# Four full-precision passes for two blocks of three early steps, x batches one step later, and two wide warming products

## The reference, cut to what matters

```python
def layer(x, adj, W, b):            # x 8192x128, adj 8192x8192, W 128x128, all float32
    h = jnp.maximum(_layernorm(x, axis=-1), 0.0)
    support = jnp.matmul(h, W)
    out = jnp.matmul(adj, support) + b
    return x + jax.nn.relu(out)
```

## Time and profile before

| | us |
|---|---|
| median of 3 runs | 722.28 (722.16 to 722.79) |
| the profiled execution | 722.6 |
| its span, first to last instruction | 720.8 |
| PE busy | 715.5 (99%) |
| PEld busy | 586.4 (81%) |
| DVE busy | 620.4 (86%) |
| ACT busy | 517.0 (72%) |
| POOL busy | 171.5 (24%) |
| DMA | 281.60 MB, mean 391 GB/s |

### The profile page before, as it was taken

The page is one execution under the profiler, slowest core; times in us unless marked ns, Lnnn a source line. Parts: engine busy times, 40 slices in busy tenths (PEclk is TensorE's granted clock), DMA queues, the critical chain, the costliest instruction groups (busy, mean ns, idle before and its releaser), DMA issues.

```text
span 720.8 us, 7916 instructions
## 1 busy us (share of the span) xinstructions
PE 715.5 (99%) x3125; PEld 586.4 (81%) x3125; DVE 620.4 (86%) x387; ACT 517.0 (72%) x394; POOL 171.5 (24%) x99
## 2 busy tenths in 40 slices
PE   9999999999999999999999999999999999999998
PEld 5788888888888888888888888888888888888886
DVE  5899999999999888988789888878888787888885
ACT  2798988888888867766567677677676676766662
POOL 4445455554444402222011000000000000033213
PEclk9999999999999999999999999999999999999999
DMA  9999999999999999999999999999999999999992
GB/s 352 408 409 407 408 412 415 412 416 415 416 414 416 418 415 412 398 374 402 373 412 392 408 409 389 377 401 383 386 392 373 389 394 387 391 404 397 366 400 85
DMA packets 45109, 281.60 MB, mean 391 GB/s; under 512 B 5136, under 2 KB 5776, under 8 KB 31504
## 3 DMA queue, kind: packets, MB, share of 16 engines
q1 hardware_dynamic: 44496, 280.25, 97.5%
q10 hardware_dynamic: 576, 0.85, 0.4%
HBM read 276.89 MB, written 4.19 MB: 390 GB/s over the span
## 4 chain that ended last, share of the span: by engine, by line
PE 97%; DMA 2%; DVE 0%; ACT 0%; SPq 0%; issue 0%; DVEq 0%
PE banks L558 94%; DMA raw<-adj 2%; PE banks L600 2%; PE banks L592 1%; PE banks L585 0%; PE banks L586 0%; PE banks L584 0%; ACT high L378 0%; SPq L244 0%; DVE x_sb L479 0%; DVE x_sb L487 0%; DVEq L150 0%; DVE warm L491 0%; DVEq L478 0%
## 5 line engine op out<-in xcount | busy, mean ns | idle before, releaser
L516 DVE TENSOR_TENSOR low<-raw,high 128x3072 fp32r<-128x3072 f32 (+2 forms) x255 | 574.7, 2276 | 86.4 <-PE banks L558 64.4
L378 ACT ACTIVATE high<-raw 128x3072 fp32r<-128x3072 f32 (+2 forms) x255 | 483.0, 1903 | 190.3 <-DMA raw<-adj 178.4
L558 PE MATMUL banks<-high,h_high 128*128 128x512 f32 x1012 | 271.6, 390 | 1.1 <-ACT high L378 1.1
L558 PE MATMUL banks<-high,h_low 128*128 128x512 f32 x1012 | 271.0, 389 | 0.0
L558 PE MATMUL banks<-low,h_high 128*128 128x512 f32 x1012 | 267.8, 389 | 0.0
L558 PEld LDWEIGHTS banks<-high,h_high 128*128 128x128 f32 x1012 | 189.8, 188 | 41.8 <-ACT high L378 2.0
L558 PEld LDWEIGHTS banks<-low,h_high 128*128 128x128 f32 x1012 | 189.8, 188 | 39.9 <-DVE low L516 0.4
L558 PEld LDWEIGHTS banks<-high,h_low 128*128 128x128 f32 x1012 | 189.9, 188 | 39.5
L330 POOL TENSOR_SCALAR x_sb<-x_sb,bias 128x512 f32<-128x512 f32 x16 | 49.5, 3095 | 419.3 <-DMA x_sb<-x_blocks 419.3
L321 POOL TENSOR_SCALAR z_sb<-x_sb,neg_mean,rstd 128x128 f32<-128x128 f32 x60 | 89.8, 1510 | 1.6
L306 POOL TENSOR_TENSOR rstd<-var_eps,minus_half 128x4 f32<-128x4 f32 (+2 forms) x17 | 31.6, 1861 | 118.3 <-DVE var_eps L421 109.1
(11 more groups left out here) (34 smaller groups left out, 50.1 us busy)
## 6 DMA issues: line engine op xcount, KB each, us to landing
raw<-adj SPq DMA_DIRECT2D x106, 1536.0 KB, 8.9
raw<-adj SPq DMA_DIRECT2D x82, 768.0 KB, 10.5
raw<-adj SPq DMA_DIRECT2D x69, 512.0 KB, 11.8
x_sb<-x_blocks SPq DMA_DIRECT2D x16, 256.0 KB, 8.6
out_blocks<-x_sb SPq DMA_DIRECT2D x15, 256.0 KB, 9.7
x_sb<-x SPq DMA_DIRECT2D x14, 256.0 KB, 11.9
raw<-adj SPq DMA_DIRECT2D x3, 256.0 KB, 6.9
raw<-adj ACTq DMA_DIRECT2D x1, 256.0 KB, 2.7
```

What stands on the lines that cost most here:

```text
L378: nc.scalar.activation(high[:, t % HIGH_SLOTS, cols], raw[:, t % RAW_SLOTS, cols], ACT.Copy).then_inc(high_ready, 1)
L516: nc.vector.tensor_tensor(low[:, t % LOW_SLOTS, cols], raw[:, t % RAW_SLOTS, cols], high[:, t % HIGH_SLOTS, cols].bitcast(F32), ALU.subtra ...
L558: return nc.tensor.matmul(banks[:, FIRST_BANK[g] + c, :], h[:, (t - FIRST_STEP[g]) * DEPTHS[g] + k, :], tile[:, slot, at:at + BANK], start ...
```

## The change

Six things change. In steps 5, 6 and 7 (`PART_WHOLE`) the third piece (blocks 4 and 5) is no longer halved by ACT and DVE (`halves_of` leaves it out of both loops and of the counts in `halved`); PE multiplies it raw by the whole tile in f32 (`with_whole`), between low 0 and low 1. The whole tiles 5 to 7 are made by one new DVE operation at the end of step 2, `h_part`, from `z_sb`. SP, when it loads into the slots of steps 5 to 7 (at steps 9 to 11), waits also for PE. Batches of x are loaded, and their means taken, at steps 6, 10, ... in place of 5, 9, ...; the squares move to steps 7 and 8, 11 and 12, ..., the variance to 8, 12, ...; batch 3 is rectified at step 5 in place of 7, and the later ones where they were. The halving of `h_first` moves from step 9 to step 28. The warming products are two of 448 columns in place of eight of 128, from a buffer that `last_sum` lends; ACT's first activation reads `minus_half` and waits for POOL in place of DVE.

```diff
@@ -35,7 +35,9 @@
-WARMING = 8
+
+PART_WHOLE = range(5, 8)
+WARMING, WARM = 2, 448
@@ -88,11 +90,16 @@
+def halves_of(t):
+
+    return range(len(split_of(t)) - (t in PART_WHOLE))
+
+
 def halved(t, i=None):
 
     while len(HALVED_BEFORE) <= t:
-        HALVED_BEFORE.append(HALVED_BEFORE[-1] + len(split_of(len(HALVED_BEFORE) - 1)))
-    return HALVED_BEFORE[t] + (len(split_of(t)) if i is None else i + 1)
+        HALVED_BEFORE.append(HALVED_BEFORE[-1] + len(halves_of(len(HALVED_BEFORE) - 1)))
+    return HALVED_BEFORE[t] + (len(halves_of(t)) if i is None else i + 1)
@@ -107,23 +114,24 @@
 def mean_at(t):
-    return batch_at(t, 1, 3) if t >= 5 else None
+    return batch_at(t, 2, 3) if t >= 6 else None
 
 
 def variance_at(t):
-    return batch_at(t, 3, 3) if t >= 7 else None
+    return batch_at(t, 0, 2) if t >= 8 else None
 
 
 def rectified_at(t):
-    return 2 if t == 2 else batch_at(t, 3, 2) if t >= 7 else None
+
+    return {2: 2, 5: 3}.get(t, batch_at(t, 3, 2) if t >= 11 else None)
 
 
 def squares_at(t):
 
-    j = batch_at(t, t % 4, 3) if t >= 6 and t % 4 in (2, 3) else None
-    if j is None:
+    j = batch_at(t, 3, 3) if t % 4 == 3 else batch_at(t, 0, 2)
+    if t < 7 or j is None:
         return None
-    at = BATCHES[j][0] + (t % 4 - 2) * 2
+    at = BATCHES[j][0] + (t % 4 == 0) * 2
     return j, range(at, at + 2)
@@ -268,6 +280,9 @@
+                if t - RAW_SLOTS in PART_WHOLE:
+
+                    sp.wait_ge(products_done, t - RAW_SLOTS + 1)
@@ -314,6 +329,8 @@
+                if j == 4:
+                    pool.wait_ge(h_part_ready, 1)
@@ -359,8 +376,8 @@
-            act.wait_ge(warm_ready, 1)
-            nc.scalar.activation(unread[:, :], warm[:, 0:1], ACT.Square)
+            act.wait_ge(constants_ready, 1)
+            nc.scalar.activation(unread[:, :], minus_half[:, 0:1], ACT.Square)
@@ -510,19 +527,25 @@
+                if t == 2:
+
+                    dve.wait_ge(products_done, 1)
+                    tiles = len(PART_WHOLE)
+                    nc.vector.tensor_scalar(h_part[:, 0:tiles * P], z_sb[:, x_slot(2) % Z_SLOTS, P:(1 + tiles) * P],
+                                            0.0, None, ALU.max).then_inc(h_part_ready, 1)
...
-                if t == 9:
+                if t == 28:
@@ -589,7 +612,7 @@
             for _ in range(WARMING):
-                nc.tensor.matmul(banks[:, PSUM_BANKS - 1, 0:P], warm[:, :], warm[:, :], start=True, stop=True)
+                nc.tensor.matmul(banks[:, PSUM_BANKS - 1, 0:WARM], warm[:, 0:P], warm[:, :], start=True, stop=True)
@@ -632,17 +655,29 @@
+
+                def with_whole(i):
+                    pe.wait_ge(h_part_ready, 1)
+                    pe.wait_ge(raw_landed[t % RAW_SLOTS][i], landed(t, i))
+                    at = (t - PART_WHOLE[0]) * P
+                    for c in blocks_of(t, i):
+                        nc.tensor.matmul(banks[:, FIRST_BANK[0] + c, :], h_part[:, at:at + P],
+                                         raw[:, t % RAW_SLOTS, c * BANK:(c + 1) * BANK], start=False, stop=False)
 
 
                 with_high(0)
                 if len(pieces) == 3:
                     with_high(1)
                     with_low(0)
-                    with_high(2)
-                    with_low(1)
-                    with_low(2)
+                    if t in PART_WHOLE:
+                        with_whole(2)
+                        with_low(1)
+                    else:
+                        with_high(2)
+                        with_low(1)
+                        with_low(2)
```

More of the change, by code:

```diff
@@ L170, in gnn_layer @@
         rstd = sb("rstd", [P, TILES])
-        warm = sb("warm", [P, P])
         unread = sb("unread", [P, 1])
@@ L183, in gnn_layer @@
         last_sum = sb("last_sum", [P, BANK])
+        warm = last_sum[:, 0:WARM]
+        h_part = last_sum
         banks = ctx.enter_context(nc.psum_tensor("banks", [P, PSUM_BANKS, BANK], F32))
@@ L197, in gnn_layer @@
         h_first_ready = sem("h_first_ready")
+        h_part_ready = sem("h_part_ready")
         early_high = sem("early_high")
@@ L374, in _ @@
                     act.wait_ge(high_used, t - HIGH_SLOTS - FOUR_PASS + 1)
-                for i in range(len(split_of(t))):
+                for i in halves_of(t):
                     cols = columns_of(t, i)
@@ L379, in _ @@
                                          ACT.Copy).then_inc(high_ready, 1)
-                    if i == (0 if t >= NARROW_UNTIL else len(split_of(t)) - 1) and rectified_at(t) is not None:
+                    if i == (0 if t >= NARROW_UNTIL else halves_of(t)[-1]) and rectified_at(t) is not None:
                         rectify(rectified_at(t))
@@ L625, in with_high @@
                             last = product(t, c, k, h_low, high, t % HIGH_SLOTS)
-                    if i == pieces[-1]:
+                    if i == halves_of(t)[-1]:
                         last.then_inc(high_used, 1)
```

## The result

| | before | after |
|---|---|---|
| median of 8 runs, us | 722.42 (722.15 to 722.79) | 726.51 (723.68 to 728.84) |
| the profiled execution, us | 722.6 | 728.84 |
| its span, us | 720.8 | 727.0 |

The change makes the kernel slower: ratio 1.0057, interval 1.0043 to 1.0071. The forecast was 722.1 us and no change, the range ended at 723.3. The runs also scatter over 5 us where those of before lie within 0.7.

What follows compares the result with a forecast made beforehand. PE was taken to bound the kernel. The terms +1.06 - 1.3 - 0.29 + 0.3 = -0.23 us gave 722.4 on the profiled 722.6 us, or 722.1 us against the median; range 721.4 to 723.3.

Steps and rivals of the forecast that it cites:

- What bounds the kernel, and the prize: PE is the bound; its stalls in steps 5 and 10 make the prize at most 1.6 us out of 722.
- Four passes, +1.06 us: Steps 5 to 7, last two blocks: six products of 0.858 us replace 0.681 us each, +1.06 us on PE.
- The step-5 stall, -1.3 us: Step 5: piece 2 is read as it lands, so PE's whole stall goes, -1.3 us.
- rival 1: Step 6: a lagging DMA engine makes piece 1 0.4 to 1.2 us late; 722.6 to 723.3 us, chance 0.15.
- `h_part` on DVE, +0.3 us: Ahead of step 3's subtractions: the new DVE operation reaches PE nearly whole, +0.3 us, bounds 0 and 0.8.
- The step-10 stall, -0.29 us: Step 10: PE's 0.29 us lost on low products goes, as the copies of h_first leave step 9.
- Warming: Kernel start: two wide products end before h_first is there; costs nothing if the clock still rises in time.
- Rival 2: Kernel start: the clock rises late, first products 0.86 us slower each; chance 0.09, 0.06 of it beyond two products.
- Moved steps: Statistics one step later: ACT waits some 0.5 us every fourth step, nothing on the path.
- Rival 3: Rectified tiles make PE wait or ACT hands its 0.5 us on; 722.1 plus 0.5 to 4.5 us, chance 0.04.

Runs made afterwards that it cites:

- a1: The changed kernel with x batches, means, squares and variances back at their old steps; 722.56 us, ratio 1.0005.
- w2: The changed kernel with the old schedule, four passes in step 5 alone and the eight narrow warming products; 721.95 us, ratio 0.9995.
- w1: The changed kernel with the old schedule and four passes in step 5 alone, wide warming kept; 722.04 us, ratio 1.0001.
- h1: The changed kernel with only the first 64 columns of each piece subtracted on DVE in steps 24 to 63; 722.50 us, ratio 1.0005.
- v1: The changed kernel with all four squares and the variance back at steps 7, 11, ..., loads and means left late; 722.89 us, ratio 1.0012.
- p2: The changed kernel with each DVE subtraction of steps 24 to 63 cut into two of half the width; 722.59 us, ratio 1.0008.
- a3: The changed kernel with rectification behind the last piece of its step, not the first, from step 24 on; median 725.2 us, ratio 1.0038.

## Why the prediction was wrong, by its own steps

- **What bounds the kernel, and the prize: right.** PE, two stalls of 1.6 us; both are gone. (Rows 3 hold two more waits of weight loads for ACT, 0.3 and 0.2 us before 20 us, which the prediction passed over.)
- **Four passes, +1.06 us: right.** The records of the new product stand 0.43 us apart, as in step 1, without a cost for entering or leaving them: the fourth starts at 31.87 us (from the same view), and the second product behind it at 32.53, which is 0.43 + 0.23 us later.
- **The step-5 stall, -1.3 us: right in its size; which part removed it is open.** The packet of instructions moved as the prediction thought it might: it lies between 28 and 30 us before and between 32 and 34 us in the changed kernel, where nothing waits for it. In a1 it has moved too, so that a1 has no wait there doesn't single out the four passes. With the wide warming alone (g1) it lies between 30 and 32 us, step 5 has no stall, and PE stands 0.60 us in step 6 instead. Nothing came in step 6 of the changed kernel (rival 1), but rival 1's waits are real in g1 and w2.
- **`h_part` on DVE, +0.3 us: right in kind.** The instruction took 0.35 us, and of that 0.17 reached PE in step 3.
- **The step-10 stall, -0.29 us: right.**
- **Warming: nothing, about right.** The memset of 448 columns took 0.43 us and the first real product came 0.35 us later, hidden behind the landing at 8.5 us. Rival 2's mechanism is real (9.79 us in w1) but isn't what made this change slow.
- **Moved steps: this is the step that failed.** It read POOL's batch as 8.0 us long, moved it by one step, found ACT waiting 0.5 us and called that covered, since ACT is busy 72% of the time. Its first half held: 0.57 us. Two things were wrong. The first is that POOL's time is not its own. Four instructions of 0.44 us take 5.4 us or more because DVE's subtractions hold them off, so where the batch meets DVE's pauses is part of its price, and a step's shift changes it. The second is that the wait lies in a closed lap. The prediction compared one end of POOL with one rectification and never added the lap up: with POOL's 8.0 us it would have come to 15.9 us, 0.4 short of PE's four steps, and not to a cover of a quarter of ACT's time. ACT's idle time is mostly waiting for DMA (178 us in all before, 152 in the changed kernel), and DVE's pauses follow from it. When ACT waits for POOL and then catches up, pauses close and POOL gets slower: the wait is 0.57, 0.88, 2.98, then 4.36 us, the lap 16.1, 17.8, then 17.5 us, and what it has above 16.3 us PE pays as soon as the pieces made ready ahead are used up. The rows for this stood in the trace: instructions of 0.44 to 3.6 us of one form; the prediction weighed such a hold for one instruction of DVE and not for the sixty of POOL.
- **Rival 3** named the wait, with 722.6 to 726.6 us, and the moved steps had "0.5 us for each of some nine batches" if the cover failed. The measured 726.5 lies in that, by luck: neither POOL's growth nor the lap was in it, and it cost some 1.1 us for six batches. Its chance of 0.04 was the mistake of the numbers: with ACT's margin gone from 3.5 us to -0.5 by the prediction's own sum, it deserved much more, and the range had to reach it.

The Trainium skill (SBUF - State Buffer, SBUF: two separate sides) says that an instruction of DVE with two SBUF inputs and one of GpSimd exclude each other on a shared port pair for their whole length. The trace agrees in the main, by h1 (1.75 against 7.00 us), though no run singles out the ports as the reason. Beyond it, the rows show one POOL instruction taking as long as three subtractions in a row.

## What to carry to other kernels

Before a chain of small work on GpSimd is moved, compare its instructions' longest and shortest times: where they differ widely, as 3.6 and 0.44 us did here, its length belongs to VectorE's pattern at the new place, not to the old one. A margin that turns negative on an engine with idle time is not covered by that idle time if the idle time stands elsewhere in the cycle. Look for what is queued behind the wait: if the input of the next round is, the chain is closed, and its whole lap has to be shorter than what the bounding engine does in a round. Leave room for what catching up does to the pauses that others live on. And a change of several parts whose gain is under 0.1% should have its schedule moved by itself first: here one part cost 4 to 8 us and the others together nothing that can be measured.

## What the hardware showed that I had not expected

- A POOL instruction of 0.44 us beside back-to-back subtractions takes three of them: 5.11 us with 1.70, 2.7 us with 0.9 (v1, p2), and 3.5 us in the wide steps, where one takes 1.17.
- The same program gives two clusters of times, 722.3 to 723.2 and 727.3 to 728.2 us in a3, at the same clock.
- The granted clock rose at 4.5 and 4.6 us in the profiled runs of the two kernels, but at 6.1, 7.6 and 9.8 us in others of nearly the same program (g1, p2, w1). The first halved product came at 15.33 us in both kernels, and at 15.74, 16.16 and 17.54 us in these.
